# A two-layer graph kernel on one core: the adjacency for the second layer loaded by whole rows, x1 reloaded in sixteen pieces, one logarithm in the finish, and the first two row tiles of the mean in sequence

## What is computed

```
h = relu(layernorm(x))
x = x + attention(h, adj)        # scores = (a + 2 adj) * mask, softmax over a row, times values
h = relu(layernorm(x))
x = x + hyperbolic_layer(h, adj, W):
    XW    = mobius_matvec(W, h)                  # a point per row, with norms, artanh, tanh
    gamma = max(2 / (1 - |XW|^2), 1e-15)
    nom, denom, alpha = adj @ (gamma XW), adj @ (gamma - 1), row sums of adj
    a_mean = (nom/denom) / (1 + sqrt(1 - |nom/denom|^2))
    AXW   = tanh(alpha * artanh(|a_mean|)) * a_mean / |a_mean|
    out   = expmap0(relu(logmap0(AXW)))          # logmap0 takes artanh(|AXW|) again, clipped below 1
```

## Time and profile before

| | us |
|---|---|
| median of three runs (lowest, highest) | 861.0 (859.3, 863.12) |
| profiled execution | 860.4 |
| its span | 858.6 |
| PE busy | 754.5 (88%) |
| DVE busy | 664.4 (77%) |
| ACT busy | 491.3 (57%) |
| POOL busy | 47.7 (6%) |
| DMA queue of SP (q1), share of 16 engines | 68.8% |

### The profile page before, as it was taken

One profiled execution on the slowest core, in us unless ns is written; L12 is line 12 of the kernel. 1 busy time (PEld: TensorE's weight loads), 2 busy tenths in 40 slices (PEclk: granted clock), 3 DMA queues, 4 the chain that ended last, 5 costly groups with the idle time before them and its releaser, 6 DMA issues.

```text
span 858.6 us, 15125 instructions
## 1 busy us (share of the span) xinstructions
PE 754.5 (88%) x4989; PEld 693.8 (81%) x4996; DVE 664.4 (77%) x1370; ACT 491.3 (57%) x897; POOL 47.7 (6%) x96
## 2 busy tenths in 40 slices
PE   5999789999999999994665889999999999999780
PEld 4888677787778888783565889999999999999780
DVE  6778668878877888775585568888888888888865
ACT  2444366677776777676562335555555555555774
POOL 0000011000101000000000000000000000000340
PEclk9999989999999999998786999999999999999995
DMA  5115376776677776635409989999899889989631
GB/s 136 50 57 214 134 283 228 287 286 230 229 259 255 279 287 235 227 103 120 95 1 219 245 182 199 184 185 186 179 183 184 180 179 180 181 178 186 134 113 49
DMA packets 53373, 157.13 MB, mean 183 GB/s; under 512 B 9040, under 2 KB 30800, under 8 KB 47184
## 3 DMA queue, kind: packets, MB, share of 16 engines
q1 hardware_dynamic: 53328, 156.60, 68.8%
HBM read 148.16 MB, written 8.42 MB: 182 GB/s over the span
## 4 chain that ended last, share of the span: by engine, by line
PE 62%; DVE 15%; DMA 7%; SPq 4%; issue 4%; ACT 4%; DVEq 3%; ACTq 0%
PE bank L591 47%; PE bank L702 8%; DMA adjL<-in_adj 3%; DVE least L1420 3%; DMA adjU<-in_adj 2%; DVE adjT_lo L1360 2%; SPq L419 2%; PE bank L688 2%; PE bank L657 2%; DVE least L1404 2%; SPq L483 1%; DVE X_lo L1338 1%; DVE bank L1352 1%; DVE v L1221 1%; PE bank L583 1%
## 5 line engine op out<-in xcount | busy, mean ns | idle before, releaser
L591 PE MATMUL bank<-X_hi,adjT_hi 128*128 128x258 f32 x1024 | 296.1, 289 | 36.6 <-DVE adjT_lo L1360 36.6
L591 PE MATMUL bank<-X_hi,adjT_lo 128*128 128x258 f32 x1024 | 294.1, 287 | 0.0
L591 PE MATMUL bank<-X_lo,adjT_hi 128*128 128x258 f32 x1024 | 294.0, 287 | 0.0
L591 PEld LDWEIGHTS bank<-X_hi,adjT_hi 128*128 128x128 f32 x1024 | 198.9, 194 | 39.4 <-DVE adjT_lo L1360 26.2
L591 PEld LDWEIGHTS bank<-X_lo,adjT_hi 128*128 128x128 f32 x1024 | 199.4, 195 | 0.0
L591 PEld LDWEIGHTS bank<-X_hi,adjT_lo 128*128 128x128 f32 x1024 | 199.0, 194 | 0.0
L909 ACT CAST adjT_hi<-bank 128x1024 fp32r<-128x1024 f32 x96 | 97.4, 1014 | 131.5 <-PE bank L591 88.5
L1352 DVE STREAM_TRANSPOSE bank<-adjL 128x1024 f32<-128x1024 f32 x96 | 119.6, 1246 | 36.2 <-DMA adjL<-in_adj 36.1
L1360 DVE TENSOR_TENSOR adjT_lo<-bank,adjT_hi 128x1024 fp32r<-128x1024 f32 x96 | 116.1, 1210 | 16.7 <-ACT adjT_hi L909 16.4
L702 PE MATMUL bank<-values,probT 128*128 128x256 f32 x512 | 121.2, 381 | 4.9 <-ACT probT L945 4.8
L702 PEld LDWEIGHTS bank<-values,probT 128*128 128x128 f32 x512 | 93.2, 190 | 18.7 <-ACT probT L945 7.2
(11 more groups left out here) (168 smaller groups left out, 1119.8 us busy)
## 6 DMA issues: line engine op xcount, KB each, us to landing
adjL<-in_adj SPq DMA_DIRECT2D x128, 512.0 KB, 9.1
adjU<-in_adj SPq DMA_DIRECT2D x32, 1024.0 KB, 5.7
adjL<-in_adj SPq DMA_DIRECT2D x16, 2048.0 KB, 10.0
x_scratch<-x SPq DMA_DIRECT2D x16, 258.0 KB, 3.5
xin<-in_x SPq DMA_DIRECT2D x8, 512.0 KB, 3.8
xt<-in_x SPq DMA_DIRECT2D x16, 256.0 KB, 3.3
x_all<-x_scratch SPq DMA_DIRECT2D x4, 1024.0 KB, 17.6
out_x<-res SPq DMA_DIRECT2D x8, 512.0 KB, 2.9
```

Of the source, the lines that this page charges most:

```text
L591: last = pe.matmul(dst, a[i][a_cols], b[j][b_cols], start=(k_first and n == 0), stop=(k_last and n == 2))
```

## The change

Four edits.

1. `adj_q` is cut otherwise: `mean_adj` still issues four DMAs a tile, each 512 KB, but DMA i now takes the 32 whole rows 32*i to 32*i + 31 and fills the piece s = i of all 128 partitions. On the HBM side its view counts 4 column quarters (4 KB apart) outermost, then 32 rows (16 KB apart), then 1024 contiguous floats; on the SBUF side 128 partitions, then 1024 floats. The data end in the same places.
2. x1 comes back in sixteen DMAs of two row tiles (256 KB) each: `x1_back(0)` and `x1_back(1)` after the loads of tiles 2 and 3, and then one after every second load of a tile. POOL and DVE wait for all sixteen before they add x1.
3. The finish leaves out the second pair of Ln and Tanh: artanh of the tanh is replaced by the minimum of its argument and FURTHEST. `finish_product`, one `finish_series` and `finish_log` go.
4. FIRST_CHUNKS takes the four chunks of tile 0, then the four of tile 1.

```diff
+FURTHEST = math.atanh(1.0 - 2.0 ** -23)
-FINISH_FUNCTIONS = [(ACT.Sqrt, "squares", "roots"), (ACT.Ln, 5, 5), (ACT.Tanh, 2, 2), (ACT.Ln, 5, 5),
-                    (ACT.Tanh, 1, 3)]
-FINISH_CHUNKS = (1, 2, 4, 5, 7)
+FINISH_FUNCTIONS = [(ACT.Sqrt, "squares", "roots"), (ACT.Ln, 5, 5), (ACT.Tanh, 1, 3)]
+FINISH_CHUNKS = (1, 2, 4)
...
-    FIRST_CHUNKS = [(t, q) for q in range(NQ) for t in range(2)]
+    FIRST_CHUNKS = [(t, q) for t in range(2) for q in range(NQ)]
...
-    adj_q = adj.rearrange("(t s r) (a f) -> t a r s f", s=QD, r=RB, a=QD)
+    adj_q = adj.rearrange("(t s r) (a f) -> t s a r f", s=QD, r=RB, a=QD)
...
             def mean_adj(t, par):
-                for a in range(QD):
-                    sp.dma_start(adjL_q[a * RB:(a + 1) * RB, par], adj_q[t, a]).then_inc(d_adj[par], 16)
+                for i in range(QD):
+                    sp.dma_start(adjL_q[:, par, i], adj_q[t, i]).then_inc(d_adj[par], 16)
...
+            def x1_back(i):
+                sp.dma_start(x1_all_2[:, i], x1_pairs[i]).then_inc(s_x1_all, 16)
+
             for t in range(2):
                 mean_adj_next(t, t)
-                for part in range(2 * t, 2 * t + 2):
-                    sp.dma_start(x1_all[:, part * HT // 2:(part + 1) * HT // 2, :],
-                                 x1_dram[part * N // 4:(part + 1) * N // 4, 0:D].rearrange("(t p) d -> p t d", p=P))\
-                      .then_inc(s_x1_all, 16)
+                x1_back(t)
+
             with sp.Fori(1, HT - 1) as i:
                 for par in range(2):
                     mean_adj_next(2 * i + par, par)
+                x1_back(i + 1)
...
-            pool.wait_ge(s_x1_all, 16 * 4)
+            pool.wait_ge(s_x1_all, 16 * HT)
...
             def finish_scaled(c):
                 artanh_end(V[2][:, c], V[5][:, c], V[6][:, c], V[7][:, c])
-                tt(V[2][:, c], V[2][:, c], alpha[:, c], ALU.mult).then_inc(s_f, 1)
-            def finish_product(c):
...
-            def finish_log(c):
...
+                tt(V[2][:, c], V[2][:, c], alpha[:, c], ALU.mult)
+                dve.drain()
+                dve.scalar_tensor_tensor(out=V[0][:, c], in0=V[2][:, c], scalar=FURTHEST, in1=V[0][:, c], op0=ALU.min,
+                                         op1=ALU.mult)
                 dve.drain()
                 tt(V[1][:, c], V[0][:, c], roots[:, 2, c], ALU.mult)
                 dve.drain()
...
-            FINISH_PARTS = (finish_root, finish_mean, finish_series, finish_scaled, finish_product, finish_series,
-                            finish_log, finish_exp)
+            FINISH_PARTS = (finish_root, finish_mean, finish_series, finish_scaled, finish_exp)
...
-            dve.wait_ge(s_x1_all, 16 * 4)
+            dve.wait_ge(s_x1_all, 16 * HT)
```

More of the change, by code:

```diff
@@ L1 @@
+import math
 import concourse.bass as bass
@@ L98, in graph_layers_kernel @@
         x1_dram = nc.dram_tensor("x1_scratch", [N, XW], F32, kind="Internal").ap()
+        x1_pairs = x1_dram.rearrange("(i j p) d -> i p j d", j=2, p=P)[:, :, :, 0:D]
         x1_halves = x1_dram.rearrange("(h s p) d -> s p h d", p=P, h=2)
@@ L216, in graph_layers_kernel @@
         x1_all = place("x1_all", [P, T, D], "qx")
+        x1_all_2 = x1_all[:, :, :].rearrange("p (i j) d -> p i j d", j=2)
         qx_v = qx[:, :, :].rearrange("p (g j) c -> p g j c", j=BPC)
@@ L1559, in finish_scaled @@
                 artanh_end(V[2][:, c], V[5][:, c], V[6][:, c], V[7][:, c])
-                tt(V[2][:, c], V[2][:, c], alpha[:, c], ALU.mult).then_inc(s_f, 1)
-            def finish_product(c):
-                function_done()
-                tt(V[0][:, c], V[0][:, c], V[2][:, c], ALU.mult)
+                tt(V[2][:, c], V[2][:, c], alpha[:, c], ALU.mult)
                 dve.drain()
[L1567 to L1572, removed]
-            def finish_log(c):
-                artanh_end(V[2][:, c], V[5][:, c], V[6][:, c], V[7][:, c])
-                tt(V[0][:, c], V[0][:, c], V[2][:, c], ALU.mult)
+                dve.scalar_tensor_tensor(out=V[0][:, c], in0=V[2][:, c], scalar=FURTHEST, in1=V[0][:, c], op0=ALU.min,
+                                         op1=ALU.mult)
                 dve.drain()
```

## The result

The changed kernel took 1135.51 us (median of four runs, 1134.62 to 1135.85) beside 860.15 for the kernel before: ratio 1.3193, 95% interval 1.3156 to 1.3229. The profiled span is 1133.8 us. The sign was forecast and the number of working engines too; the size was not (1,582).

A forecast was written before the change was run, and what follows sets the result against it. PE was taken to bound the steady mean before, adj's loads after: 483 us to tile 2's load, 1,049 for 30 loads, 11 for x1, 38 for the last tile, 1.8 around the span: 1,582 us, range 1,080 to 1,820.

The forecast's parts named there:

- The bound of the kernel before: In the steady mean PE is the bound: 836 matmuls in 100 us, 11.5 us a tile, DMA with 8% to spare.
- Four engines: In the mean's adj loads, the HBM side's outermost counter of 4 leaves four of sixteen engines working; chance 0.81.
- The rate of the four: In the mean's adj loads, each engine was taken at 15 GB/s, between 12.5 and 27.0: 35.0 us a tile.
- the 12.5 of the loads before: GB/s for each of 16 engines in the mean's old loads, which write 32 partitions each; the forecast's lower rate.
- The sum: Whole span: 483 to tile 2's load, 1,049 for 30 loads, 11 for x1, 38 for the last tile: 1,581 us.
- the attention's 27.0: GB/s an engine in the attention, where a load spans 128 partitions; the forecast's upper rate, 19.4 us a tile.
- My rival of four engines that don't meet: In the mean's loads, four engines run at 20 to 27.0 GB/s each: 1,087 to 1,302 us; chance 0.26.
- The transition: Between attention and mean, small transfers land behind adj loads: points_root at 458, 24.3 us of DVE work, tile 2's load at 483.
- Loads back to back, two buffers no help: In the mean, each load is issued while the one before is still on its way: 30 loads by 35.0 us.
- The finish: After the last matmul 4.8 us less; among the last four tiles at most 2.5 us back if PE is the bound.
- Edit 2: x1's pieces between adj loads: 11 us in all instead of 18 in the hole; no cost if PE were the bound.
- Edit 4: At the mean's start, three more chunks (8.6 us) follow the last points, covered by the next load's 35 us.

The follow-up runs named there:

- g_all_rows: Changed kernel with each of a tile's four DMAs taking 1024 columns of all 128 rows, output leaving the reference: 833.31 us, ratio 0.9703 to the kernel before.
- f_quarters: Changed kernel with each group of 32 whole rows loaded as four DMAs of 32 partitions and 128 KB: 834.4 us, ratio 0.9702 to the kernel before.
- h_two: Changed kernel with each group of 32 rows loaded as two DMAs of 64 partitions, 2 outermost on the HBM side: 1782.99 us, run once.
- s_halves: Changed kernel plus four bursts of two-partition DMAs (32 apart in 1 and 3, 64 in 2 and 4), mean loads on 64 partitions: 934.14 us, bursts included.
- d_finish_only: Kernel before with only the finish changed (second pair of Ln and Tanh left out): 850.61 us, ratio 0.9891.
- a_adj_only: Kernel before with only the loads of adj changed to 32 whole rows per DMA: 1144.37 us, ratio 1.3305.

## Why the prediction was right in its mechanism and wrong in its size

- **The bound of the kernel before**: right. With sixteen engines at work and 355 GB/s to a full share (g_all_rows) the mean stays at PE's 837 matmuls in 100 us.
- **Four engines**: right, shown by the share of 0.26 to 0.28, by f_quarters (same rows, 32 outermost, 834 us) and by h_two (half the share, twice the time a tile).
- **The rate of the four: this is the step that failed.** I took 15 GB/s an engine, nearer to the 12.5 of the loads before, "and engines that start together could meet at the same place". It measured 25.0 GB/s: 20.98 us a tile with its share of x1 instead of 35.0 and x1's 0.4. The sum had 483 for the issue of tile 2, then 1,049 + 11 for the loads; it was 460.72, and 1093.36 - 460.72 = 632.6. These are 427 us of the 446 missed; the earlier issue is 22, and the last tile took 40.4 us instead of 38. The range holds the result because it spans both rates; the point stood on the slower one, and rates of 20 GB/s or more had a chance of only 0.26. The meeting is real (s_halves), but the four don't start together. After the issue at 383.23 the first pieces of adj start at 384.97, 385.24, 385.26 and, on the fourth engine, 387.22. By then one engine has begun seven pieces and two have begun two each. The windows of the changed kernel read:

```profile
386.00:387.00 1.00, 1.00 (x6) 0.87 (x6) 0.91 (x3) 0.00 (x0) 0.00 (x0) 1.00 0.18 25
387.00:388.00 1.00, 1.00 (x8) 0.77 (x6) 0.85 (x5) 0.00 (x0) 0.00 (x0) 1.00 0.22 90
388.00:392.00 4.00, 0.76 (x5) 0.58 (x4) 2.94 (x18) 2.98 (x11) 0.00 (x0) 1.00 0.26 103
```

  They come to their full rate only four to five microseconds after the issue, and from then on a piece of 4 KB takes 0.16 us in the median in the changed kernel and in h_two, against 0.33 in the loads before. An engine that is several pieces behind another writes other partitions of its 32, and in burst 1 of s_halves the disturbance is weaker where one engine is ahead by a little. That the late start is what keeps the four apart fits both runs, but no run forced them into step with the changed loads, and the trace does not say which engine wrote which partitions, so it is argued and not shown. The loads before differ in this: sixteen engines inside one group of 32 can't step aside.
- **The row that I should have taken** is the attention's 27.0. The 12.5 belongs to sixteen engines crowding 32 partitions; I gave its weight to the piece size, and g_all_rows shows that 4 KB pieces run at 22 GB/s an engine. My rival of four engines that don't meet said 1,087 to 1,302 and holds the result.
- **The transition**: right in its links. The small transfers waited behind the adjacency's, points_root to the last points_low took 24.3 us again, and the load of tile 2 came right behind it. By the same rate all of it came earlier: points_root at 436.32 instead of 458.
- **Loads back to back, two buffers no help**: right, thirty waits of DVE, one a tile.
- **The finish**: 4.8 us at the end right (4.7); among the last tiles 3.7 us instead of at most 2.5, where PE is the bound (d_finish_only).
- **Edit 2**: the direction right, 9 us instead of 15 or more when alone. Between the loads of four engines a piece costs more than the 0.8 us of the sum: 20.98 us a tile against the 20.34 of a_adj_only, 0.64 for half a piece, about 18 us for fourteen pieces instead of 11. **Edit 4**: nothing, right.

## What to carry to other kernels

Before a DMA is reshaped, read off both sides' outermost counter: in these runs the smaller one decided how many of the sixteen engines worked, with the same bytes and the same pieces. Where a layout forces a small one, cut the DMA so that the rows come outermost on both sides (sixteen DMAs of 128 KB a tile took the kernel to 834 us, four of 512 KB to 1,136). And price the engines that are left by a row in which nothing crowds them, not by the row that looks most alike.

## What the runs showed of the hardware that was not expected

- A DMA for four engines also takes SP longer to issue: 6.55 us for four of them at 383.23, where the loads before took 1.92; in h_two eight DMAs for two engines take 26.63 us at 383.07. The engines begin one after another, over 2.3 us in the changed kernel.
- Two engines, one writing partition r and one partition r + 32, share about the bandwidth of one (25 to 33 GB/s, 1.21 us for most pieces of 16 KB); with r + 64 they have about twice as much (41 to 57 GB/s, 0.61 us a piece).
- Four small DMAs of 32 partitions each do better than one DMA with four pieces for each of 32 partitions: 245 GB/s at full share against 200, and 297 when the two halves of the partitions take turns.
